# Layer two: the next expert's gate and up weights split chunk by chunk, inside the last tile of a block

## What is computed

```python
def _L1_ffn_ref(inputs, w1, w3, w2):
    B, T, D = inputs.shape
    E = w1.shape[0]
    C = T // E
    x = inputs.reshape(B, E, C, D)
    gate = jnp.einsum('becd,edf->becf', x, w1)
    up = jnp.einsum('becd,edf->becf', x, w3)
    h = jax.nn.silu(gate) * up
    out = jnp.einsum('becf,efd->becd', h, w2)
    return out.reshape(B, T, D)
...
    x = x + s * g
    xn = _layernorm(x, axis=-1)
    s = _L1_attn_ref(xn, ...)
    g = _silu(_L1_ffn_ref(xn, L1_ffn_w1, L1_ffn_w3, L1_ffn_w2))
    x = x + s * g
```

## Time and profile before

| | |
|---|---|
| median of 3 runs | 4390.36 us (4386.61 to 4394.35) |
| the profiled execution | 4401.49 us, its span 4399.7 us |
| mean granted clock of TensorE | 0.978 of full speed |
| TensorE busy over the span | 4125.3 us (94%) |
| VectorE | 2703.7 us (61%) |
| ScalarE | 1936.3 us (44%) |
| GpSimd | 1696.7 us (39%) |

### The profile page before, as it was taken

The page is one execution under the profiler, slowest core; times in us unless marked ns, Lnnn a source line. Parts: engine busy times, 40 slices in busy tenths (PEclk is TensorE's granted clock), DMA queues, the critical chain, the costliest instruction groups (busy, mean ns, idle before and its releaser), DMA issues. The chain is left out here.

```text
span 4399.7 us, 72682 instructions
## 1 busy us (share of the span) xinstructions
PE 4125.3 (94%) x28636; PEld 3270.7 (74%) x28636; DVE 2703.7 (61%) x5040; ACT 1936.3 (44%) x3576; POOL 1696.7 (39%) x1337
## 2 busy tenths in 40 slices
PE   8699999999999998899999999999995999999995
PEld 8656656656656655798898988888895888888884
DVE  7467777777777776344434343444432688888885
ACT  2134444444444444445444444545442444444441
POOL 2234334334334332444434444444433234444443
PEclk9999999999999998999999999999997999999998
DMA  9501011011011010333323232332224344454433
GB/s 313 168 25 35 30 39 35 30 40 35 30 40 35 30 40 20 92 49 59 62 42 65 47 61 43 66 51 57 43 40 98 98 102 110 100 116 112 106 68 43
DMA packets 254003, 294.21 MB, mean 67 GB/s; under 512 B 21600, under 2 KB 226656, under 8 KB 251616
## 3 DMA queue, kind: packets, MB, share of 16 engines
q0 software_dynamic: 88064, 117.74, 15.8%
q1 hardware_dynamic: 165600, 171.82, 12.1%
HBM read 155.15 MB, written 134.35 MB: 66 GB/s over the span
## 5 line engine op out<-in xcount | busy, mean ns | idle before, releaser
L564 DVE TENSOR_TENSOR e_hTl<-e_hf,e_hTh 128x512 fp32r<-128x512 f32 x512 | 354.6, 692 | 800.5 <-ACT e_hTh L506 752.2
L1077 POOL TENSOR_TENSOR a_mix<-a_tmp,a_h 128x512 f32<-128x512 f32 x320 | 389.9, 1238 | 793.8 <-PE ps L1376 745.1
L425 POOL DMA_INDIRECT acc_d<-e_y,e_sids x256 | 409.0, 1598 | 707.4 <-DVE e_y L580 654.6
L505 ACT ACTIVATE e_hf<-ps_heads,e_b 128x512 f32<-128x512 f32 x512 | 355.4, 694 | 677.3 <-PE ps_heads L663 620.8
L663 PE MATMUL ps<-e_w2h,e_hTh 128*128 128x256 f32 x2048 | 578.8, 283 | 0.0
L663 PE MATMUL ps<-e_w2h,e_hTl 128*128 128x256 f32 x2048 | 577.3, 282 | 0.0
L663 PE MATMUL ps<-e_w2l,e_hTh 128*128 128x256 f32 x2048 | 571.3, 279 | 1.0 <-issue 1.0
L663 PE MATMUL ps_heads<-e_xTh,e_w1h 128*128 128x512 f32 x1024 | 418.4, 409 | 16.2 <-ACT e_hTh L506 8.8
L663 PE MATMUL ps_heads<-e_xTh,e_w1l 128*128 128x512 f32 x1024 | 405.5, 396 | 0.0
L663 PE MATMUL ps_heads<-e_xTl,e_w1h 128*128 128x512 f32 x1024 | 405.4, 396 | 0.0
L663 PEld LDWEIGHTS ps<-e_w2h,e_hTh 128*128 128x128 f32 x2048 | 385.7, 188 | 20.4
(11 more groups left out here) (293 smaller groups left out, 9218.0 us busy)
## 6 DMA issues: line engine op xcount, KB each, us to landing
r_x<-in_L_attn_hidden_states SPq DMA_DIRECT2D x32, 512.0 KB, 6.2
xn_d<-r_xn SPq DMA_DIRECT2D x32, 512.0 KB, 4.8
xnT_d<-r_xT SPq DMA_DIRECT2D x32, 512.0 KB, 3.8
acc_d<-a_zeros POOLq DMA_DIRECT2D x32, 512.0 KB, 3.0
s_d<-a_s SPq DMA_DIRECT2D x32, 512.0 KB, 2.8
e_w<-in_L_ffn_w SPq DMA_DIRECT2D x16, 1024.0 KB
f_a<-acc_d SPq DMA_DIRECT2D x32, 512.0 KB, 3.8
f_x<-s_d SPq DMA_DIRECT2D x32, 512.0 KB, 5.2
```

The costliest lines, as they stand in the source:

```text
L425: pool.indirect_dma_start(acc_d, bass.IndirectOffsetOnAxis(ap=sids[:, GT * q + t:GT * q + t + 1], axis=0), ys[r][:, t, :], None, compute_o ...
L505: nc.scalar.activation(hf[m % 2][:], ps[2 + m % 2][:], ACT.Gelu, bias=b1s[:, m:m + 1])
L564: nc.vector.tensor_tensor(hT[q % 2][1][:, m, :], hf[m % 2][:], hT[q % 2][0][:, m, :].bitcast(F32), ALU.subtract).then_inc(h_sb, 1)
L1077: nc.gpsimd.tensor_tensor(mix[n][:, m, :].rearrange("p (c t) -> p c t", c=GT), tmp[i % 2][:].rearrange("p (c t) -> p c t", c=GT), h[q % 2] ...
```

## The change

`split_up` is cut into the six chunks of `m`, on both engines. In the last tile of a block, ScalarE copies chunk `m` of w1 (and of w3 for `m` < 5) right behind `high_h(g, m)`, and VectorE takes the differences right behind the scan steps of chunk `m`. `up_split` and `up_high` count chunks instead of tiles, and TensorE waits for the chunk that it is about to use. `split_down` stays where it is. The split ahead of the first tile is cut up too, with nothing between the chunks. The wait of SP is the same one in the new count.

```diff
@@ SP, tile
-                        sp.wait_ge(up_split, j + 1)
+                        sp.wait_ge(up_split, FC * j + 1)
@@ VectorE
-            def split_up(j):
-                dve.wait_ge(up_high, 2 * j + 2)
-                low(w1p[1][:], w1s[:], w1p[0][:])
-                low(w3p[1][:], w3s[:], w3p[0][:]).then_inc(up_split, 1)
+            def split_up(j, m):
+                dve.wait_ge(up_high, FC * j + m + 1)
+                cols = slice(m * P, (m + 1) * P)
+                done = low(w1p[1][:, :, cols], w1s[:, :, cols], w1p[0][:, :, cols])
+                if m < FC - 1:
+                    done = low(w3p[1][:, :, cols], w3s[:, :, cols], w3p[0][:, :, cols])
+                done.then_inc(up_split, 1)
@@ VectorE, tile
+                renewed = q == QB - 1 and not last
                 if q == 0:
                     split_down(j)
                 for m in range(FC):
...
                     if scans:
                         scan_part(*scans, q, m, 1, None)
+                    if renewed:
+                        split_up(j + 1, m)
                 if not last:
                     turn(g + 1)
-                    if q == QB - 1:
-                        split_up(j + 1)
@@ ScalarE
-            def split_up(j):
+            def split_up(j, m):
 
                 act.wait_ge(up_in, 48 * j + 48)
-                nc.scalar.copy(w1p[0][:], w1s[:]).then_inc(up_high, 1)
-                nc.scalar.copy(w3p[0][:], w3s[:]).then_inc(up_high, 1)
+                cols = slice(m * P, (m + 1) * P)
+                done = nc.scalar.copy(w1p[0][:, :, cols], w1s[:, :, cols])
+                if m < FC - 1:
+                    done = nc.scalar.copy(w3p[0][:, :, cols], w3s[:, :, cols])
+                done.then_inc(up_high, 1)
@@ ScalarE, tile
                     high_h(g, m)
                     if m == 1 and not ending:
                         gate_in(i, k + AHEAD)
+                    if q == QB - 1 and not last:
+                        split_up(j + 1, m)
                 if not last:
                     turn(g + 1)
-                    if q == QB - 1:
-                        split_up(j + 1)
                 gate_out(g, k, first)
@@ TensorE, tile
                 drive(g)
-                if q == 0:
-                    pe.wait_ge(up_split, j + 2)
                 for m in range(FC):
+                    if q == 0:
+                        pe.wait_ge(up_split, FC * j + m + 2)
                     up(g, m, begin)
```

More of the change, by code:

```diff
@@ L1985, in _ @@
             centre(0)
-            split_up(0)
+            for m in range(FC):
+                split_up(0, m)
             turn(0)
```

## The result

The changed kernel takes 4394.36 us (median of 15 runs, 4387.70 to 4399.76), the kernel before 4386.47 (15 runs, 4378.88 to 4394.35) beside it. The ratio is 1.0019, with a 95% interval of 1.0011 to 1.0027: 8 us slower, 0.19%. By the forecast's own line for what can be told from no change (0.2%, 8.8 us) this is still "the same"; the interval leaves zero out.

The account below looks back on a forecast made before the run. VectorE's work up to `f_xTl`, then `drive` and one chunk, was taken to set the tile. Six steady boundaries at +2.1 us and the first at +5.4 gave +18 us on 4390.4: 4408 us, range 4381 to 4420.

Parts of the forecast that it names:

- The loop that sets a tile: VectorE's work from first multiply to `f_xTl` (23.1 us), then `drive` and one chunk (4.6 us): 27.7 us; added VectorE work lengthens it.
- The eleven pieces: In a block's last tile, eleven VectorE differences of 256 elements at 0.33 us each cost 3.6 us, 4.6 without overlap.
- GpSimd: In the last tile, pieces of chunks 1 and 3 wait for GpSimd's multiplies: 1.5 us a tile, between 0 and 2.6.
- The last tile as a whole: What a block's last tile pays on VectorE: 5.2 us, in block 0 4.4 us.
- What the boundary gives back: From `f_xTl` to the first multiply, 10.4 us becomes 5.85: 4.6 us back at steady boundaries, 0.5 at the first.
- The low clock: TensorE's clock is low in `drive` after last-tile stalls, so the first multiply comes 7.3 us after `f_xTl` instead of 5.85.
- first rival: TensorE's clock holds at the boundaries: +0.6 us at each steady one, +3.9 at the first, +7.5 us, 4398 us; 25%.
- third rival: VectorE's pieces take only its idle time beside TensorE's work, so boundaries keep their gain: 28 us less, 4362 us; 10%.

Follow-up runs that it names:

- low_late: Changed kernel with VectorE's eleven w1 and w3 differences, still cut, moved back behind the last tile's turn; ratio 0.9969 to the kernel before, 13.6 us less.
- no_low: Changed kernel without the low parts of w1 and w3 for experts 1 to 7 (77 differences left out); ratio 0.9942 to the kernel before, 25 us less.
- low_aside: Changed kernel with the pieces of chunk 1 put behind chunk 2 and of chunk 3 behind chunk 4; ratio 1.0008 to the kernel before.
- second profile: The changed kernel run again unchanged, on another chip; ratio 1.0019 to the kernel before.
- cut_w2_behind: Kernel with copies and differences behind the turn in three pieces per weight, w2 difference moved behind the next tile's first low part; 0.9950 to the kernel before.
- filled: Changed kernel with eight useless TensorE matmuls ahead of the transposes in each block's last tile; ratio 1.0019 to the kernel before.
- low_late_whole: `low_late` with two whole differences of w1 and w3 instead of eleven pieces, TensorE waiting for both; ratio 0.9980 to the kernel before.
- cut_pool_late: Kernel with chunked copies and differences behind the turn, plus GpSimd's two f_xd multiplies waiting for VectorE's first multiply; ratio 0.9967 to the kernel before.

## Why the direction was right and the size wrong

- **The loop that sets a tile.** Right. VectorE is busy from the first multiply to `f_xTl` for all but 1.0 us in the kernel before and in the changed one (22.2 of 23.1 us, 27.2 of 28.2), and the tile grew by what was put on it; TensorE, as full as VectorE before, has 4.6 us to spare now. The experiments that moved or removed only the pieces (`low_late`, `no_low`) took the last tile from 32.7 to 28.2 us, with everything else in place.
- **The eleven pieces.** 0.34 us from start to start, forecast 0.33; as durations 0.41 to 0.42. The rule of the Trainium skill ("VectorE: DVE Perf Modes", the section on the fixed extra latency of SBUF sources) gives 0.42 us for 256 elements, which the rows show as the duration; as a cost per piece it would have been too high by about a quarter. (By it the forecast would have been some 8 us higher, not 7: seven times 1.1.)
- **GpSimd.** Right in place (chunks 1 and 3) and near in size: 1.50 and 1.48 us where 0.42 is plain, and `low_aside` shortened the steady last tiles by 1.0 to 1.3 where 1.5 had been counted. The last tile as a whole: +5.0 us measured at the six later blocks, 5.2 forecast; block 0 +3.8 (+4.1 in the second profile), 4.4 forecast. Summed over seven, the last tiles paid 33.7 us where the forecast had 35.6.
- **What the boundary gives back.** Right where the clock holds: 5.8 us from the start of `drive` to the first multiply, forecast 5.85 from `f_xTl`.
- **The low clock.** This term of the sum failed. It was counted at all seven boundaries with 1.45 us each, 10 us. Measured: three of seven in one profile and two in the other, at 0.8 to 1.3 us each, so 3.1 and 1.8 us. The argument ran from single waits (1.50 us kept the clock, 1.78 lost it) to a sequence of waits of 5.6 us in 10. The waits came where the forecast had them and each a little shorter (1.83, 0.80, 1.38 and 0.59 us, 4.6 in all), but the clock behind such a sequence falls at some boundaries only, and in part so early that it is back at 1.00 by `drive`. With 3 us in place of 10 the sum of the forecast is 11 us, inside the measured interval of 4.8 to 11.8.
- **What the argument could have seen.** It took the clock from the length of the first matmul behind a wait, 0.79 us low and 0.50 high. That sign fails in the kernel before: behind two of its six waits of 3.82 us the first matmul takes 0.50 or 0.51 us, and the clock falls only about 1 us later:

```profile
3632.46 0.51 PE L2122 MATMUL ps_heads<-f_xTh,f_w1h 128*128 128x512 f32 x1 [3.82 <-DVE f_w3l L1842]
```
```profile
3632.46:3633.26 0.80, 0.80 (x3) 0.67 (x4) 0.80 (x1) 0.00 (x0) 0.80 (x1) 1.00 0.00 0
3633.26:3637.26 4.00, 4.00 (x12) 3.13 (x11) 2.13 (x3) 0.60 (x1) 0.28 (x1) 0.57 0.00 0
```

So even behind one and the same long wait the moment of the fall shifts from boundary to boundary, and how much of the low stretch lands on `drive` was open. The windows of the earlier trace rows, of one boundary, did not show it.

- **Luck.** The first rival's 7.5 us is close to the measured 8.7 of the tiles only because two errors cancel: the clock cost 3.1 us where the rival had none, and the last tiles paid 1.9 us less than counted.
- **The third rival, pieces that fit in beside TensorE's work,** is ruled out: the last tiles grew by 5.0 us, and VectorE had 1.0 us free where the pieces needed 3.6. That `cut_w2_behind` comes to 22.6 us under before is another mechanism, since its pieces stand behind `f_xTl`.

Not tried: a second pair of buffers for the parts of w1 and w3, so that the differences could stand in the 4.6 free microseconds of the tiles before. No run here shows whether the phase has the room in SBUF for it.

## What to carry to other kernels

When two engines hand work to each other in a loop and both look full, find the stretch of the loop in which the engine that is to do the extra work waits for the other by design (here VectorE's 4.6 us behind `f_xTl`), and put it there: with the same eleven pieces the kernel is 8 us slower than before when they stand ahead of that stretch and 18 us faster when they stand in it. Cut a large preparation so that the consumer can start on the first piece; what that bought here is mostly that TensorE has no single long wait and keeps its clock, for which VectorE would have to wait in turn. A stall that is removed at one place is only gained if no engine of the loop gets the work that was hidden behind it.

## What was not expected of the hardware

- TensorE's clock behind several waits of about a microsecond. In the last tiles of the six later blocks, waits of 1.8 to 1.9, 0.8, 1.4 and 0.6 us within 10 us were followed by the low level (1.2 GHz) at `drive` in three cases of six in the first profile and two in the second, by a low stretch of some 4 us that ended before `drive` in one and one, by none in the rest. With the first wait filled (`filled`), the other three were followed by it at `drive` in four of six.
- The clock behind one wait: it stayed at 1.00 behind 1.50 us, fell behind 1.78 us, at four of six boundaries behind 2.5 us (`low_late_whole`), and at six of six behind 3.8 us (the kernel before), at two of these six only about 1 us after the matmuls had started again.
- A held-up operation costs the rest of GpSimd's multiply however small it is: 256 elements took 1.48 to 1.52 us in place of 0.42 beside multiplies of 1.3 to 1.4 us each. The Trainium skill ("SBUF — State Buffer", on contention and the shared port pair) says that the later of a VectorE operation with two SBUF inputs and a GpSimd operation that reads SBUF waits for the whole of the other; the rows of `cut_pool_late` agree (1.34 and 0.85 us in place of 0.45), down to the operation with a PSUM input that is not touched (0.68 us).
